# Normalising the attention output through DRAM instead of on TensorE, and a new table of places

## Chip, cores and metric

The kernel runs on one core of a Trainium2 chip. The metric is device time in microseconds (us) of one execution.

## What is computed

Six transformer layers on 4 images of 512 tokens with 256 channels and 16 heads of 16 channels, and then a mixture of 8 experts. Cut to what matters:

```python
for i in range(6):
    xn = adaln(x, cond, n1)                 # layer norm, scale and shift
    q, k, v = split(xn @ qkv_w[i].T)
    a = attn(rope(q), rope(k), v)           # softmax(q k / 4) v, head by head
    x = x + a @ so_w[i].T
    xn = adaln(x, cond, n2)                 # the same with keys and values from the context
    x = x + attn(rope(xn @ cq), rope(ctx @ ck), ctx @ cv) @ co_w[i].T
    xn = adaln(x, cond, n3)
    x = x + gelu(xn @ f1_w[i].T + f1_b[i]) @ f2_w[i].T + f2_b[i]
x = x0 + x
out = x + moe(layernorm(x))                 # top 2 of 8 experts, at most 640 rows each
```

The softmax is computed without its division: `attn` first yields, for each head, the sums of exp(score) times value and the plain sum of exp(score), and the quotient of the two is the attention output.

## The kernel before

A job is one image in one attention (self or cross): 8 jobs a layer, 48 in all. The program runs in slots; slot k works on four jobs at once. **Pass 1** of job k: 32 pairs of score products (`pass1`, L788), whose row maxima DVE takes (`maximum`, L999). **Pass 2** of job k-1: 64 shifted score products (`pass2`, L761), of which ACT takes the exponential (L837), and the value products (`pv`, L774), which gather four heads at a time in one bank (`psv`): each head has 32 rows, 16 of value sums, then one row (row 16) that is the sum of exp. ACT copies a finished group of four heads to `osum` (`copy_group`, L845). The **tail** of job k-2: quotient, output projection, addition to x. The **head** of job k+1: norm, projections to q, k, rotation, split into three bf16 parts, a trip through DRAM (`bounce`) and the loads of the stacked operands `qstack` and `kstack`.

A slot has 32 places, numbered 0 to 31, two for each of its 16 units. In a unit PE issues pass2, pass1 twice, pass2, the chunks of the even place, pass2, pv, pass2, the chunks of the odd place. A **chunk** is a piece of tail or head work that goes through one PSUM bank, `side`; there is only one such bank, so a chunk starts when the one before has been read. `SHORT_PLACES` and `LONG_PLACES` say at which place each chunk stands: `HV` value projection, `HT` transposes of the normed rows, `HQ`, `HK` projections; `T1`, `T2`, `O` the tail; in long slots (tails of cross attention, 4 slots in 8, where the feed-forward network follows) also `LT`, `F1`, `F2`. All engines run through the places in the same order, in program order on each.

The tail before: `T1`, four chunks, transposes `osum` (four 128x128 transposes each, L663); DVE takes reciprocals of the sums of exp and multiplies (L1018, L1019) into `anat`. `T2`, two chunks, transposes `anat` back (L663), ACT copies to `aT` (L890, shown in rows as `hT`, whose memory it shares). `O`, two chunks, projects (L677), DVE adds to x (L1048).

SP issues all DMAs of the layers, one after another, waiting in line for each. At the turn of a slot it waits until pass 2 of job k-1 is complete, then issues ten DMAs: the second half of the heads of `qstack` and `kstack` for the next job (`load_first(k + 1, 1)`, L515 and L517, `load_second(k + 1, 1)`, L526). They read DRAM:

```python
if j >= 2:
    sp.wait_ge(s_p2full, place.jobs(j - 2, 64) + 32 * (hf + 1))
```

`NORM_PLACES` says where DVE computes the norm: for `HT` the statistics at places 0 and 1, the Newton step at 3, the four normed tiles at 3, 3, 4, 4 (L989).

In the experts, PARTS are 16 halves of experts (384 and 256 rows). For a part, `gather_T` transposes its rows on PE, DVE copies them to `gT` (`read_T`, L1466), `hidden` multiplies by w1 (L1299), ACT applies gelu, `outputs` multiplies by w2 (L1315).

Of the kernel before, what the change touches and what calls it, by code (L numbers as in the profile page):

```python
# [29 lines left out]
P = 128  # L30
# [51 lines left out]
CHUNKS_PER_LAYER = 200  # L82
DVE_PER_LAYER = 196
# [216 lines left out]
def layers(nc, a, x, mod, ident, identb, eps, maskrow, rows, acc, s_pad):  # L300
    with ExitStack() as ctx:
# [20 lines left out]
        anat = sb("anat", [P, TT, D])  # L322
# [6 lines left out]
        nT = anat[:, :, :].rearrange("p (k a) n -> p k (a n)", k=KD)  # L329
# [6 lines left out]
        recip = sb("recip", [P, TT, H])  # L336
# [6 lines left out]

        bounce = [nc.dram_tensor(f"bounce{i}", (NPROD, D, S), BF16, kind="Internal").ap() for i in range(2)]
# [26 lines left out]

        s_full = sem("chunk_filled")
# [23 lines left out]
        def slot_chunks(k):  # L396
# [14 lines left out]
            if tail:  # L411
                put("T1", "T2", "O")
# [49 lines left out]
        def _(sp):  # L462
# [27 lines left out]

            def write_part(j, w, part):
# [97 lines left out]
        def _(pool):  # L589
# [44 lines left out]
            def slot(k, p2, p1, tail, head):  # L634
                if head:
# [15 lines left out]
        def _(pe):  # L651
# [29 lines left out]
            def side_work(k, what, c):  # L681
                if what == "T1":
                    if c == 0:
                        pe.wait_ge(s_os, place.jobs(k - 1, 4))
                    transposes(begin(k, what, c), [osum[:, g, c * P:(c + 1) * P] for g in range(4)])
                elif what == "T2":
                    if c == 0:
                        wait_read(pe, place, k, "T1", 2)
# [862 lines left out]
```

## Time and profile before

| | |
|---|---|
| time, median of 3 runs | 4453.81 us (4446.65 to 4462.31) |
| profiled execution, its own time | 4442.28 us |
| its span | 4440.6 us |
| mean granted TensorE clock | 0.962 |
| layers' slots (first pass2 to the last) | 177.8 to 4069.8 us |
| experts' loop on PE | 4246.5 to 4423 us |

The span runs from the first to the last instruction. PE is TensorE, PEld its weight loads, DVE VectorE, ACT ScalarE, POOL GpSimd, SP SyncE. A slot k begins with its first pass2 product (L761). In a row of the timeline the number in brackets is the idle time of the engine before the instruction, and what ended it. In the rows `anat` also stands for `nT`, and `hT` also for `xnat` and `aT`, which share their memory.

### The profile page before, as it was taken

How to read it: one execution, taken by the hardware profiler on the slowest of the kernel's cores; microseconds unless marked ns; L12 is line 12 of the kernel's file. 1: busy time of each engine (PE TensorE's matmuls, PEld its weight loads, DVE VectorE, ACT ScalarE, POOL GpSimd, SP SyncE). 2: the span in 40 equal slices, each digit the busy share in tenths (PEclk: the TensorE clock that was granted, in tenths of full speed). 3: DMA queues.
4: the chain of work that ended last, by engine and by line, in shares of the span. 5: the costliest groups of instructions: out<-in, count | busy, mean ns of one | idle time of the engine just before them, and what ended most of it. 6: DMA issues, size and time to landing. Idle time of an engine off the chain costs nothing. (4 is left out here: it accounts for less than half of the span.)

```text
span 4440.6 us, 68492 instructions
## 1 busy us (share of the span) xinstructions
PE 3940.5 (89%) x20630; PEld 1833.7 (41%) x20630; DVE 2907.1 (65%) x4711; ACT 2561.9 (58%) x4302; POOL 857.7 (19%) x518
## 2 busy tenths in 40 slices
PE   3699999999999999999999999999999999997467
PEld 1233344533344533345433345433345433354355
DVE  3777766677766678766678766678766677752311
ACT  1376656667666567666567665567666566654122
POOL 4312121112121112211111211111211121200133
PEclk7799999999999999999999999999999999999689
DMA  5354323244323244332244332244332344410234
GB/s 162 85 135 108 97 69 78 63 108 120 87 78 72 60 113 119 87 80 65 67 108 116 94 72 66 68 108 116 97 75 59 74 129 111 109 30 13 83 99 95
DMA packets 271578, 396.39 MB, mean 89 GB/s; under 512 B 28312, under 2 KB 218400, under 8 KB 270880
## 3 DMA queue, kind: packets, MB, share of 16 engines
q1 hardware_dynamic: 263904, 382.18, 34.1%
q0 software_dynamic: 7296, 9.51, 1.3%
q8 instruction: 196, 3.21, 0.3%
q14 instruction: 182, 1.49, 0.1%
HBM read 226.63 MB, written 170.67 MB: 89 GB/s over the span
## 5 line engine op out<-in xcount | busy, mean ns | idle before, releaser
L837 ACT ACTIVATE prob<-ps 128x512 f32<-128x512 f32 x3072 | 1768.2, 596 | 1225.2 <-PE ps L761 1207.6
L999 DVE TENSOR_REDUCE negmax<-ps 128x2 f32<-128x1024 f32 x1536 | 1836.7, 1219 | 217.6 <-PE ps L788 195.2
L761 PE MATMUL ps<-qstack,kstack 114*128 114x512 bf16 x3072 | 1162.4, 389 | 100.1 <-ACT prob L837 84.8
L774 PE MATMUL psv<-prob,v 128*32 128x512 f32 x6144 | 829.5, 612 | 0.0
L761 PEld LDWEIGHTS ps<-qstack,kstack 114*128 114x128 bf16 x3072 | 284.6, 97 | 1190.3 <-ACT prob L837 794.5
L616 POOL TENSOR_TENSOR rot<-ropep 128x512 f32<-128x512 f32 x96 | 122.5, 1276 | 2486.7 <-DVE ropep L1032 2467.7
L788 PE MATMUL ps<-kstack,qstack 49*128 49x512 bf16 x3072 | 496.8, 388 | 97.9 <-DVE negmax L999 76.8
L736 PE MATMUL side<-anat,wf 128*128 128x256 f32 x1536 | 377.1, 388 | 9.9 <-DVE hT L1037 8.9
L1037 DVE TENSOR_SCALAR hT<-side,f1b 128x256 f32<-128x256 f32 x384 | 168.2, 479 | 303.6 <-PE side L736 303.6
L747 PE MATMUL side<-wf,hT 128*128 128x256 f32 x1536 | 347.9, 379 | 2.8 <-DVE x L1044 1.6
L736 PEld LDWEIGHTS side<-anat,wf 128*128 128x128 f32 x1536 | 285.6, 192 | 65.7 <-DVE hT L1037 30.9
L747 PEld LDWEIGHTS side<-wf,hT 128*128 128x128 f32 x1536 | 291.9, 190 | 41.6 <-issue 2.4
L788 PEld LDWEIGHTS ps<-kstack,qstack 49*128 49x128 bf16 x3072 | 100.0, 94 | 457.5 <-issue 279.2
L625 POOL TENSOR_TENSOR low<-rot,parts 128x1024 bf16<-128x1024 f32 x96 | 204.7, 2132 | 379.0 <-ACT parts L876 379.0
L619 POOL TENSOR_TENSOR rot<-rot,parts 128x1024 f32<-128x1024 f32 x96 | 205.4, 2140 | 207.3 <-ACT parts L872 207.3
L1044 DVE TENSOR_TENSOR x<-x,side 128x256 f32<-128x256 f32 x96 | 40.4, 421 | 297.5 <-PE side L747 297.5
L774 PEld LDWEIGHTS psv<-prob,v 128*32 128x32 f32 x6144 | 121.6, 109 | 272.1 <-issue 245.8
L669 PE MATMUL side<-xnT,wself 128*128 128x512 f32 x384 | 195.0, 632 | 31.1 <-DVE ropep L1032 29.2
L1048 DVE TENSOR_TENSOR x<-x,side 128x512 f32<-128x512 f32 x96 | 66.0, 688 | 171.2 <-PE side L677 171.2
L663 PE MATMUL side<-ident,hT 128*128 128x128 f32 x576 | 101.3, 303 | 82.0 <-DVE hT L989 79.5
L989 DVE TENSOR_SCALAR hT<-x,mv,y 128x256 f32<-128x256 f32 x288 | 163.9, 612 | 2.6
L1031 DVE TENSOR_TENSOR ropep<-side,cos 128x512 f32<-128x512 f32 x96 | 66.4, 692 | 137.4 <-PE side L669 98.5
(158 smaller groups left out, 3722.1 us busy)
## 6 DMA issues: line engine op xcount, KB each, us to landing
bounce<-parts SPq DMA_DIRECT2D x480, 256.0 KB, 2.5
qstack<-bounce SPq DMA_DIRECT2D x384, 192.0 KB, 5.5
kstack<-bounce SPq DMA_DIRECT2D x384, 192.0 KB, 6.1
bounce<-low SPq DMA_DIRECT2D x96, 256.0 KB, 2.1
ctxT<-in_ctxT SPq DMA_DIRECT2D x24, 512.0 KB, 3.9
nw<-in_nwT SPq DMA_DIRECT2D x18, 512.0 KB, 11.3
w<-in_w SPq DMA_DIRECT2D x16, 512.0 KB, 4.8
wself<-in_wself SPq DMA_DIRECT2D x24, 256.0 KB, 4.0
```

The lines of the kernel that those rows point to most:

```text
L619: nc.gpsimd.tensor_tensor(rot[:, :, :], rot[:, :, :], parts[w][:, 0, :, :], ALU.subtract).then_inc(s_r1, 1)
L625: nc.gpsimd.tensor_tensor(low[:, :, :], rot[:, :, :], parts[w][:, 1, :, :], ALU.subtract).then_inc(s_low, 1)
L669: mm = nc.tensor.matmul(bank, w[:, k, m * P:(m + 1) * P], act_T[:, k, :], start=(k == 0), stop=(k == KD - 1))
L736: mm = nc.tensor.matmul(bank[:, i * D:(i + 1) * D], wf1[:, kk, f * P:(f + 1) * P], nT[:, kk, th * (S // 2):(th + 1) * (S // 2)], start=(kk ...
L747: mm = nc.tensor.matmul(bank[:, 0:D], hT[th][:, f, t * P:(t + 1) * P], wf2[:, f, :], start=(f == 0), stop=(f == FT - 1))
L761: nc.tensor.matmul(ps2[:, n % RING2, :], kk[0:ROWS, h, kt * P:(kt + 1) * P], q[0:ROWS, h, :], start=True, stop=True).then_inc(s_p2full, 1)
L774: mm = nc.tensor.matmul(psv[32 * i:32 * i + 32, 0, :], v[j % 2][:, kt, (HD + 1) * h:(HD + 1) * h + 32], prob[:, 4 * (u % 2) + i, :], start ...
L788: mm = nc.tensor.matmul(ps1[:, 2 * (n % 2) + e, :], qs[j % 2][rows, 8 * e + m, t * P:(t + 1) * P], ks[j % 2][rows, 8 * e + m, :], start=Tr ...
L837: nc.scalar.activation(prob[:, 4 * (u % 2) + i, :], ps2[:, n % RING2, :], ACT.Exp, scale=HD ** -0.5).then_inc(s_prob, 1)
L989: ins = nc.vector.tensor_scalar(xnat[:, t, :], x[:, TT * (j % B) + t, :], mv[:, t, 0:1], y0[:, t:t + 1], ALU.subtract, ALU.mult)
L999: nc.vector.tensor_reduce(out_at, ps1[:, 2 * (n % 2):2 * (n % 2) + 2, :], AX, ALU.max, negate=True).then_inc(s_p1free, 1)
L1037: ins = nc.vector.tensor_scalar(hT[th][:, f, :], bank[:, i * D:(i + 1) * D], f1b[:, f:f + 1], None, ALU.add)
```

## The change

The transposes T1 and T2 go. SP writes each group of `osum` to DRAM (`value_sums`), loads the sums of exp back as `den` (128x64), and the value sums as `aT`, already in the layout that the projection wants; DVE takes one reciprocal of `den` at place 4; SP writes it to DRAM (`inverse`) and loads it back 16 times repeated (`recips`, in the memory of `nT`); POOL multiplies `aT` by it in one instruction; `O` waits for that. The rest of the chunks moves to new places. In the experts the rows of a part are transposed one part earlier than before.

```diff
 SHORT_PLACES = {
-    "HV": [1, 3], "T1": [2, 4, 5, 7], "HT": [6, 8], "HQ": [9, 10], "HK": [12, 14],
-    "T2": [15, 17], "O": [19, 21],
+    "HV": [1, 3], "HT": [6, 8], "HQ": [9, 11], "HK": [13, 15], "O": [18, 20],
 }
 LONG_PLACES = {
-    "HV": [1, 3], "T1": [2, 4, 5, 7], "HT": [6, 8], "T2": [9, 10], "O": [11, 12], "HQ": [13, 14],
-    "HK": [15, 16], "LT": [17, 18], "F1": [19, 20, 21, 22, 23, 24, 25, 26], "F2": [27, 28, 30, 31],
+    "HV": [1, 3], "HT": [5, 7], "O": [8, 10], "HQ": [9, 11], "HK": [12, 13], "LT": [15, 16],
+    "F1": [17, 18, 19, 20, 21, 22, 23, 24], "F2": [26, 27, 29, 30],
 }
-SHORT_SHIFT, LONG_SHIFT = (23, 0), (29, 0)
+SHORT_SHIFT, LONG_SHIFT = (23, 0), (28, 0)
...
-    "LT": dict(stats=[12, 12, 12, 12], aggregate=13, newton=15, tiles=[15, 15, 16, 16]),
+    "LT": dict(stats=[10, 10, 10, 10], aggregate=11, newton=13, tiles=[13, 13, 14, 14]),
 }
-GUESS_PLACES = {"HT": 2, "LT": 14}
+GUESS_PLACES = {"HT": 2, "LT": 12}
+RECIP_PLACE = 4
...
-SHORT_SPLIT = (13, 15, 18, 20)
-LONG_SPLIT = (16, 18, 20, 22)
-GELU_PLACES = (23, 27)
+SHORT_SPLIT = (13, 15, 19, 21)
+LONG_SPLIT = (13, 15, 17, 19)
+GELU_PLACES = (21, 25)
...
+            def write_sums(j, g):
+                sp.wait_ge(s_os, place.jobs(j, 4) + g + 1)
+                sp.dma_start(sums[j % 2][4 * g:4 * g + 4].rearrange("h r n -> (h r) n"), osum[:, g, :]).then_inc(s_sums, 16)
+
+            def load_attention(j):
+                sp.wait_ge(s_sums, place.jobs(j + 1, 64))
+                sp.dma_start(den[:, :], sums[j % 2][:, HD].rearrange("h (c n) -> h c n", c=P // H)).then_inc(s_den, 16)
+                for k in range(KD):
+                    sp.dma_start(aT[:, k, :], sums[j % 2][8 * k:8 * k + 8, 0:HD]).then_inc(s_aload, 16)
+                sp.wait_ge(s_recip, place.jobs(j + 1, 1))
+                sp.dma_start(inverse[j % 2].rearrange("h (c n) -> (h c) n", c=P // H), recip[:, :]).then_inc(s_inv, 16)
+                sp.wait_ge(s_inv, place.jobs(j + 1, 16))
+                for k in range(KD):
+                    sp.dma_start(recips[:, k, :], inverse[j % 2][8 * k:8 * k + 8, None, :].to_broadcast([8, HD, S])).then_inc(s_aload, 16)
...
             def slot(k, p2, p1, tail, head):
                 side_done = place.at(start[k], CHUNKS_PER_LAYER)
+                if tail:
+                    sp.wait_ge(s_full, side_done)
+                    write_sums(k - 2, 3)
+                    load_attention(k - 2)
...
                 if p2:
                     shift_rows(k, k - 1, 1)
+                    write_sums(k - 1, 0)
...
                     write_and_load(k + 1)
+                if p2:
+                    write_sums(k - 1, 1)
+                    write_sums(k - 1, 2)
...
             def slot(k, p2, p1, tail, head):        # POOL
+                if tail:
+                    pool.wait_ge(s_aload, place.jobs(k - 1, 64))
+                    nc.gpsimd.tensor_tensor(aT[:, :, :], aT[:, :, :], recips[:, :, :], ALU.mult).then_inc(s_anorm, 1)
...
                 elif what == "O":
                     if c == 0:
-                        wait_read(pe, place, k, "T2", 0)
-                        wait_read(pe, place, k, "T2", 1)
+                        pe.wait_ge(s_anorm, place.jobs(k - 1, 1))
...
                     for what, c in plan[at]:
                         side_work(k, what, c)
+                    if tail and at == RECIP_PLACE:
+                        dve.wait_ge(s_den, place.jobs(k - 1, 16))
+                        nc.vector.reciprocal(recip[:, :], den[:, :]).then_inc(s_recip, 1)
...
             gather_T(0)
             hidden(0)
+            gather_T(1)
             for n in range(len(PARTS)):
                 if n + 1 < len(PARTS):
-                    gather_T(n + 1)
                     hidden(n + 1)
+                if n + 2 < len(PARTS):
+                    gather_T(n + 2)
                 outputs(n)
```

On DVE, the rows below are from place 3's Newton step to the maxima of place 5 (`negmax<-ps`) in a slot with a tail; `hT<-x,mv,y` are the normed tiles, and an `ISA` row is a wait. Before:

```order
L984 SCALAR_TENSOR_TENSOR y<-lnv,y 128x4
L956 ISA
L989 TENSOR_SCALAR hT<-x,mv,y 128x256 x2
L997 ISA
L999 TENSOR_REDUCE negmax<-ps 128x2
L436 ISA
L1018 RECIPROCAL recip<-side 128x16
L956 ISA
L1019 TENSOR_TENSOR anat<-side,recip 128x256
L989 TENSOR_SCALAR hT<-x,mv,y 128x256 x2
L997 ISA
L999 TENSOR_REDUCE negmax<-ps 128x2
```

And of the changed kernel, on the same engine at the same place:

```order
L1011 SCALAR_TENSOR_TENSOR y<-lnv,y 128x4
L983 ISA
L1016 TENSOR_SCALAR hT<-x,mv,y 128x256 x2
L1024 ISA
L1026 TENSOR_REDUCE negmax<-ps 128x2
L1100 ISA
L1101 RECIPROCAL recip<-den 128x64
L1016 TENSOR_SCALAR hT<-x,mv,y 128x256 x2
L1024 ISA
L1026 TENSOR_REDUCE negmax<-ps 128x2
```

The wait at L1100 for `den` now stands between the maxima of place 4 and the last two normed tiles, with the maxima of place 5 behind it.

On SP, the DMAs at the turn into a slot with a tail, with what each waits for; `value_sums` is the new DRAM tensor, `hT` here the `aT` in it, `nT` the `recips`. Before, from the last of the ten loads on:

```order
L526 DMA kstack<-bounce 48x2048
L436 ISA
L561 DMA ctxT<-in_ctxT 128x2x512 [waits chunk_filled]
L439 ISA
L489 DMA qstack<-mrow 2x4x512 [waits chunk_read]
L489 DMA qstack<-mrow 2x4x512
```

And of the changed kernel:

```order
L554 DMA kstack<-bounce 48x2048
L583 ISA
L504 ISA [waits chunk_filled]
L505 DMA value_sums<-osum 128x512 [waits pv_group_copied]
L509 ISA
L510 DMA den<-value_sums 128x1x64 [waits value_sums_written]
L512 DMA hT<-value_sums 128x1x512 x2
L513 ISA
L514 DMA inverse<-recip 128x64 [waits reciprocals_ready]
L515 ISA
L517 DMA nT<-inverse 128x1x512 [waits reciprocals_written]
L517 DMA nT<-inverse 128x1x512
```

The write of the last group and the chain of loads now follow directly on the ten loads, ahead of `ctxT` and `mrow`.

On PE, from the second `HT` chunk to the first `O` chunk of a long slot of the changed kernel; `hT` is `xnat` in the first and `aT` in the last row:

```order
L703 MATMUL side<-ident,hT 128x128 x4
L790 ISA
L791 MATMUL ps<-qstack,kstack 128x512
L815 ISA
L818 MATMUL ps<-kstack,qstack 128x512 x2
L815 ISA
L818 MATMUL ps<-kstack,qstack 128x512 x2
L790 ISA
L791 MATMUL ps<-qstack,kstack 128x512
L724 ISA
L698 ISA
L717 MATMUL side<-wcross,hT 128x256 x4
```

`O` (with its wait at L724) stands at place 8, where before the second `HT` chunk stood and `O` came three places later.

## Rows read from the trace of the kernel before

**Rows 1.** The page's part 1: busy us, share of the span, instructions.

```profile
PE 3940.5 (89%) x20630; PEld 1833.7 (41%) x20630; DVE 2907.1 (65%) x4711; ACT 2561.9 (58%) x4302; POOL 857.7 (19%) x518
```

**Rows 2.** Groups of instructions by line, shapes kept apart, whole run.

```profile
L663 PE MATMUL side<-ident,osum 128*128 128x128 f32 x768 | 117.0, 274 | 3.2 <-DVE anat L1019 2.4 <-ACT osum L845 0.7
...
L663 PE MATMUL side<-ident,anat 128*128 128x128 f32 x384 | 61.5, 283 | 5.8 <-ACT hT L890 2.3 <-DVE anat L1019 0.9
...
L1018 DVE RECIPROCAL recip<-side 128x16 f32<-128x16 f32 x192 | 48.2, 251 | 35.6 <-PE side L663 35.6
```

**Rows 3.** Stretches: length, busy us of each engine (count), granted clock, DMA.

```profile
1628.60:1695.00 66.40, 62.29 (x345) 22.56 (x344) 52.40 (x74) 45.94 (x82) 13.56 (x8) 1.00 0.42 104
1926.90:2023.40 96.50, 90.95 (x481) 47.11 (x480) 64.38 (x110) 57.86 (x92) 15.87 (x9) 1.00 0.27 66
2023.40:2121.40 98.00, 92.45 (x481) 47.48 (x480) 64.39 (x110) 58.08 (x92) 15.88 (x9) 0.98 0.28 66
1556.70:1628.60 71.90, 64.05 (x344) 23.05 (x345) 51.87 (x72) 45.69 (x81) 13.54 (x8) 0.98 0.47 127
```

**Rows 4.** Timeline, PE, in the short slot that begins at 1761.4.

```profile
1767.24 0.60 PE L663 MATMUL side<-ident,osum 128*128 128x128 f32 x4
1767.68 0.38 PE L761 MATMUL ps<-qstack,kstack 114*128 114x512 bf16 x1
...
1775.37 0.39 PE L788 MATMUL ps<-kstack,qstack 49*128 49x512 bf16 x2 [0.24 <-DVE negmax L999]
...
1784.89 1.98 PE L669 MATMUL side<-xnT,wcross 128*128 128x512 f32 x4 [0.40 <-DVE ropep L1032]
```

**Rows 5.** Timeline of DVE in the same slot.

```profile
1771.69 1.23 DVE L999 TENSOR_REDUCE negmax<-ps 128x2 f32<-128x1024 f32 x1 [0.56 <-PE ps L788]
...
1773.45 0.73 DVE L989 TENSOR_SCALAR hT<-x,mv,y 128x256 f32<-128x256 f32 x2
```

**Rows 6.** Timeline of SP's DMA issues in the same slot.

```profile
1761.59 0.31 SPq L515 DMA_DIRECT2D qstack<-bounce  x1
...
1766.14 0.41 SPq L526 DMA_DIRECT2D kstack<-bounce  x1
```

**Rows 7.** Line L526 in that burst: issue to landing of its four DMAs.

```profile
DMA to landing us min/median/max: 5.1/6.0/6.9
```

**Rows 8.** Line L503 in the slot before: issue to landing, 12 DMAs.

```profile
DMA to landing us min/median/max: 2.1/2.5/2.9
```

**Rows 9.** Timeline of ACT in the same slot.

```profile
1765.12 0.59 ACT L845 ACTIVATE osum<-psv 128x512 f32<-128x512 f32 x1
```

**Rows 10.** Timeline, PE, around the long slot that begins at 1926.9.

```profile
1923.40 3.62 PE L747 MATMUL side<-wf,hT 128*128 128x256 f32 x16
...
1941.57 0.66 PE L663 MATMUL side<-ident,hT 128*128 128x128 f32 x4
...
1945.12 0.60 PE L663 MATMUL side<-ident,hT 128*128 128x128 f32 x4
...
1973.91 0.65 PE L663 MATMUL side<-ident,hT 128*128 128x128 f32 x4 [2.58 <-DVE hT L989]
```

**Rows 11.** Timeline, SP, the first of the ten loads there.

```profile
1923.60 0.31 SPq L515 DMA_DIRECT2D qstack<-bounce  x1
```

**Rows 12.** Timeline of DVE and POOL in that long slot.

```profile
1968.25 2.55 DVE L989 TENSOR_SCALAR hT<-x,mv,y 128x256 f32<-128x256 f32 x2
...
1968.47 2.19 POOL L619 TENSOR_TENSOR rot<-rot,parts 128x1024 f32<-128x1024 f32 x1 [2.04 <-ACT parts L872]
```

**Rows 13.** Timeline, DVE, first slot of a layer (begins at 1556.7).

```profile
1562.93 1.23 DVE L999 TENSOR_REDUCE negmax<-ps 128x2 f32<-128x1024 f32 x1 [5.88 <-issue]
```

**Rows 14.** Timeline of PE in the last slot.

```profile
4074.98 0.66 PE L663 MATMUL side<-ident,osum 128*128 128x128 f32 x4 [0.72 <-ACT osum L845]
...
4085.07 3.75 PE L677 MATMUL side<-wcross,hT 128*128 128x256 f32 x8 [0.78 <-ACT hT L890]
```

**Rows 15.** Groups of PE's instructions by line in the experts' loop.

```profile
L1299 PE MATMUL eps<-gT,w 128*128 128x384 f32 (+1 forms) x256 | 77.1, 456 | 20.8 <-DVE gT L1466 20.8
```

More of the change, by code:

```diff
@@ L81 @@
 FT = DFF // P
-CHUNKS_PER_LAYER = 200
-DVE_PER_LAYER = 196
+CHUNKS_PER_LAYER = 152
+DVE_PER_LAYER = 164
 EXP_SET = "natural_log_exp_and_others"
@@ L327, in layers @@
         aT = hT[0][:, 0:4, :].rearrange("p (k a) n -> p k (a n)", k=KD)
-        nT = anat[:, :, :].rearrange("p (k a) n -> p k (a n)", k=KD)
+        recips = nT
         cos = sb("cos", [P, S])
@@ L335, in layers @@
         mrow = sb("mrow", [16, 2, S], BF16)
-        recip = sb("recip", [P, TT, H])
+        den = sb("den", [P, H * S // P])
+        recip = sb("recip", [P, H * S // P])
         st = sb("st", [P, TT, 6])
@@ L342, in layers @@
         fence_at = sb("fence_at", [P, 1])
+        sums = [nc.dram_tensor(f"value_sums{i}", (H, 32, S), F32, kind="Internal").ap() for i in range(2)]
+        inverse = [nc.dram_tensor(f"inverse{i}", (H, S), F32, kind="Internal").ap() for i in range(2)]
         bounce = [nc.dram_tensor(f"bounce{i}", (NPROD, D, S), BF16, kind="Internal").ap() for i in range(2)]
@@ L370, in layers @@
         s_os = sem("pv_group_copied")
+        s_sums = sem("value_sums_written")
+        s_den = sem("probability_sums_loaded")
+        s_recip = sem("reciprocals_ready")
+        s_inv = sem("reciprocals_written")
+        s_aload = sem("attention_loaded")
+        s_anorm = sem("attention_normed")
         s_full = sem("chunk_filled")
@@ L411, in slot_chunks @@
             if tail:
-                put("T1", "T2", "O")
+                put("O")
             if p1:
@@ L681, in side_work @@
             def side_work(k, what, c):
-                if what == "T1":
+                if what == "O":
                     if c == 0:
[L684 to L688, printed above, removed]
-                        wait_read(pe, place, k, "T1", 3)
-                    transposes(begin(k, what, c), [anat[:, t, c * P:(c + 1) * P] for t in range(TT)])
-                elif what == "O":
-                    if c == 0:
-                        wait_read(pe, place, k, "T2", 0)
-                        wait_read(pe, place, k, "T2", 1)
+                        pe.wait_ge(s_anorm, place.jobs(k - 1, 1))
                     w = wcross if is_cross(k - 2) else wself
@@ L840, in copy_group @@
             def copy_group(k, j, g):
-                if g == 0 and k >= 2:
-                    wait_filled(act, place, k, "T1", 3)
+                if j > 0:
+                    act.wait_ge(s_sums, place.jobs(j - 1, 64) + 16 * (g + 1))
                 act.wait_ge(s_pv, place.jobs(j, 16) + 4 * g + 4)
@@ L887, in side_work @@
                     modulate(k, what, c)
-                elif what == "T2":
-                    wait_filled(act, place, k, what, c)
-                    nc.scalar.activation(aT[:, c, :], bank, ACT.Copy).then_inc(s_read, 1)
                 elif what == "HV":
@@ L1010, in side_work @@
             def side_work(k, what, c):
-                if what not in ("T1", "HQ", "HK", "O", "F1", "F2"):
+                if what not in ("HQ", "HK", "O", "F1", "F2"):
                     return
@@ L1014, in side_work @@
                 bank = side[:, 0, :]
-                if what == "T1":
-                    heads = bank.rearrange("p (h e) -> p h e", h=H)
-                    wait_step(step(nc.vector.reciprocal(recip[:, c, :], heads[:, :, HD])))
-                    nc.vector.tensor_tensor(anat[:, c, :].rearrange("p (h d) -> p h d", h=H), heads[:, :, 0:HD],
-                                            recip[:, c, :, None].to_broadcast([P, H, HD]), ALU.mult).then_inc(s_read, 1)
-                elif what in ("HQ", "HK"):
+                if what in ("HQ", "HK"):
                     j, w = k + 1, int(what == "HK")
@@ L1477, in biased @@
                                             b2[:, e:e + 1, :].to_broadcast([P, count, D]), ALU.add).then_inc(s_yr, 1)
+            read_T(0)
+            read_T(1)
             gates(0)
-            read_T(0)
             for n in range(len(PARTS)):
-                if n + 1 < len(PARTS):
-                    if n % 2 == 1:
-                        gates((n + 1) // 2)
-                    read_T(n + 1)
+                if n + 2 < len(PARTS):
+                    read_T(n + 2)
+                    if n % 2 == 0:
+                        gates(n // 2 + 1)
                 biased(n)
```

2 lines of the change are left out of this document (1 added, 1 removed).

## Prediction

> **What bounds the kernel.** I read the busy times first: PE is busy for 89% of the span, DVE for 65%, ACT for 58% [rows 1]. An average hides stages, so next came single slots as stretches. A short slot takes 66.4 us with PE busy for 62.3, a long one 96.5 with PE busy for 91.0 [rows 3]. The layers are bound by PE almost everywhere, and what matters is PE's order: its queue is in order, so a wait of PE for one chunk or one maximum is lost time, and work taken off PE is won time unless a wait follows. Then I read the timelines of PE, DVE, ACT and SP through the first 20 us of a slot, since there the changed kernel puts a chain of transfers.
>
> **What the removed work gives.** A T1 chunk at place 2 of a short slot starts at 1767.24 and the pass2 product after it at 1767.68 [rows 4]: 0.44 us of PE. T2's products last as long (283 ns against 274 [rows 2]). Six chunks give 6 x 0.44 = 2.64 us a slot. Also the wait of 0.40 us before the second HQ chunk goes [rows 4], since HQ now stands at 9 and 11, and the 0.24 us wait for a maximum at 1775.37 is no wait when T1's work is off DVE. Where no chunk stands between two pass2 products they must wait for ACT, for which I take back 0.2 us (a choice, below the 0.44 of the chunk gone). Without any new wait a slot would gain about 3.0 us; 46 slots carry a tail beside passes 1 and 2 of other jobs, so 138 us (slots 2 to 47).
>
> **When `den` lands.** All times are from the start of a slot; the short one begins at 1761.4.
> - The ten loads of the next job's stacks are issued from +0.2 (1761.59) to +4.7 (1766.14) [rows 6]. The last lands 6.9 us after its issue [rows 7], at +11.7; in other slots this was up to half a microsecond earlier, and I take +11.5. They are bound by data: four DMAs issued in 1.4 us land with 5.1 to 6.9 us.
> - `osum`'s last group is copied at +4.3 (1765.12 plus 0.59) [rows 9], so the write of `value_sums` is issued at about +5, right behind the loads in SP's queue. Alone such a write of 256 KB takes 2.1 us [rows 8], which would be +7. Behind the loads it cannot be earlier than these; I take +12.0 (bounds +11.7, and +13, where it takes the loads' own pace).
> - `den` is issued when the write has landed. The nearest row for its 32 KB is 2.1 us for 256 KB [rows 8]. Bounds: 1.7, as it is smaller, and 2.9. I take 2.2 with the semaphore: +14.2.
>
> In today's long slots the loads are issued 3.3 us before the slot starts (1923.60 against 1926.9 [rows 11]), because the last F2 chunk of 3.6 us stands at place 31, behind the last pass2 product [rows 10]. The new table puts it at 30, ahead of that product. So this head start goes, and long slots get the same +14.2.
>
> The Trainium skill, "DMA: Bandwidth & Descriptors", Queues, rings and completion order, says that descriptors are consumed in ring order on each DMA engine, but that completion is not FIFO per issuing engine. By the first half the write lands behind the loads, by the second it could overtake some; no row here has a DMA issued during the loads' issue that lands before them.
>
> **What waits for it.** DVE ends the maxima of place 4 at +11.4 today (1771.69 plus 1.14, the step to the next instruction at 1772.83), and 0.4 earlier without T1 at place 2: +11.0 [rows 5]. There it now waits for `den`, 3.2 us. Queued behind that wait are the last two normed tiles and the maxima of place 5. The reciprocal of 64 elements: 16 take 251 ns [rows 2]; at some 0.16 fixed and 5.5 ns each I get 0.5 (bounds 0.25 and 1.0). Two tiles 0.65 (1773.45 to the next at 1774.09), a maximum 1.13.
> - **Short slot.** The second pass1 product of unit 3 needs the maxima of place 5: 14.2 + 0.5 + 0.65 + 1.13 + 0.1 = +16.6. Today it starts at 1775.37, +14.0 [rows 4]. So PE is 2.6 us later there than today. After it come the savings not yet used: three of the six chunks (1.3) and the 0.4, less 0.2: 1.5. Net +1.1 us a slot.
> - **Long slot.** The first HT chunk, now at place 5, needs the normed tiles: 14.2 + 0.5 + 0.65 + 0.1 = +15.45. From there to place 8 are three places: two places with two small chunks take 3.55 us (1941.57 to 1945.12 [rows 10]), bare 2.65, so three bare ones 4.0, and with 0.9 for both HT chunks O is reached at +20.35. But O waits for POOL's product: the reciprocal is there at +14.7; `inverse` lands 2.2 later, +16.9; the two `recips` loads are issued 0.4 apart and land after 2.5 (median of 256 KB [rows 8]), +19.9; POOL's product of 128x1024 float32 takes 2.19 as today's L619 [rows 12]: +22.1, with semaphores +22.3. Today the second HT chunk is at this place, at +18.2 (1945.12 [rows 10]). PE is 4.1 later; one HT and two T2 chunks and 0.2 of a wait are still to be saved, 1.6. Net +2.5.
>
> The bounds together (den 1.0 earlier or 1.8 later, the transfers of `inverse` and `recips` each 0.4 less or 1 more) move a slot by about -1 to +2 us.
>
> **Other parts.** The LT wait of 2.6 us [rows 10] comes from DVE's normed tiles, which took 2.55 instead of 0.73 us while POOL ran its 2.19 us instruction [rows 12, 5]. The same instructions stay neighbours (LT 5 places behind the second O as before): nothing. The new POOL product runs when no normed tiles are due: nothing; if tiles met it, up to 1.8 a slot. The Trainium skill, "SBUF — State Buffer", section on its two separate sides, calls the pair shared by VectorE and GpSimd an exclusive lock held for the whole instruction; the row agrees, and by it POOL's product is free only between DVE's norm stages. `mrow` and `ctxT`, now issued behind the chain at about +17 instead of +10, are needed from the HK chunks on, behind HQ's second, which today starts at +23.5 (1784.89 [rows 4]): hidden. The first slot of a layer (four times; 71.9 us [rows 3]) has DVE 5.9 us late anyway [rows 13], which hides the wait: there -2.6.
>
> Last two slots: without pass 1 nothing else covers the chain. In the last one the sums are copied at 4074.98 and O starts at 4085.07 [rows 14], 10.1 later; new 2.1 + 2.2 + 0.5 + 2.2 + 2.9 + 2.3 = 12.2, so +2; the slot before reaches O with the chain still running, +4 (bounds 1 and 7).
>
> Clock: two long slots differ by 98.0 and 96.5 us, with PE's mean granted clock 0.98 and 1.00 and the waits alike [rows 3]: a spell at 1.2 GHz costs 1.4. In the first slot of a layer, after 5 us of idle, the clock is 0.98 too. PE idles 3 to 4 us at once in each new slot. I take a spell in 6 of 10 short slots and one more in half the long ones: 12 x 1.4 + 11 x 1.4 = 32 (bounds 0 and 90).
>
> Experts: PE waits 20.8 us for `gT` [rows 15]. With the rows transposed and copied one part ahead, these waits are covered by 3 to 5 us of `outputs`: -20.
>
> **Sum.** 20 short slots x 1.1 = +22; 4 first slots x -2.6 = -10; 22 long x 2.5 = +55; ends +6; clock +32; experts -20: +85. Against the profiled execution's 4442.3 us this is 4527. The median of the runs shown is 11.5 higher, so the forecast is **4539 us**.
>
> **Rivals.**
> - *Forecast: DVE waits for `den` in nearly every slot, and O in the long ones* (0.62). 4450 to 4620.
> - *`den` is in time, on the faster side* (0.16). It must land by +11, which asks that the write overtakes the loads. Then short slots win 3.0, and long ones still wait for O: 11 + 0.5 + 2.2 + 3.0 + 2.3 = +19.1, reached at 16.7, so 0.5 won. 20 x -3 - 10 - 22 x 0.5 + 6 - 20 = -95: 4359. It decides the sign as soon as `den` lands before about +12.4.
> - *The waits cost what is won* (0.12). `den` at +13: the short slots -0.1, the long ones +1.3, no clock spells: -20 - 10 + 29 + 4 - 2 = about 0: 4440 to 4467.
> - *The chain costs more* (0.10): the loads through DRAM at 5 to 7 us as the stacks' loads [rows 7], the half clock in every slot: +160 to +200, 4630.
>
> Against the first speaks nothing but the queue's order not being proven for this write; against the last, that `value_sums` and `recips` have large rows like the 2.1 to 2.9 us transfers.
>
> **Numbers.** A range of 4430 to 4610 leaves out most of the fast rival and the last: 2 in 10. What a measurement can tell from no change is 0.3%, 13 us. Slower: the forecast's 0.62, the last rival's 0.10, a third of the 0.12: 0.76. Same 0.06, faster 0.18.
>
> **What the changed profile would show.** DVE's RECIPROCAL at place 4 with 3 us of idle before it, ended by the DMA of `den`; pass1 waiting 2 to 4 us for maxima in short slots, HT for normed tiles in long ones; O's first chunk waiting about 2 us for POOL in long slots; no wait for `gT`. Short slots of 67 to 69 us, long ones of 98 to 101. The prediction is wrong if the write of `value_sums` lands before the ten loads, or if DVE reaches the reciprocal later than +14.

## The result, and the profile after

The changed kernel takes 4701.9 us (median of 4, 4696.17 to 4707.3) against 4454.35 for the kernel before in the same session (4446.65 to 4462.31): ratio 1.0555, interval 1.0531 to 1.058. The forecast was 4539 us with a range of 4430 to 4610. The sign came as forecast, and the loss is about three times as large. The profiled execution's span is 4705.6 us, so 265 us more than the 4440.6 before.

The page's part 1 of the changed kernel, busy us and share of the span:

```profile
PE 3948.3 (84%) x19478; PEld 1741.9 (37%) x19478; DVE 2832.6 (60%) x4375; ACT 2512.0 (53%) x4206; POOL 970.1 (21%) x566
```

PE has 1152 instructions fewer than in [rows 1], and is busy 7.8 us longer. The chunks that went were worth 0.44 us each in place [rows 4], 6 x 48 x 0.44 = 127 us, so the work that stayed became about 135 us slower. And PE's idle time went from 4440.6 - 3940.5 = 500 us to 4705.6 - 3948.3 = 757. These two are the loss: idle +257, slower work +135, removed work -127.

What the idle time is shows in the waits of PE (us in all, times, longest):

```profile
PE ps L791 <- ACT prob L867: 151.6, 238, 2.3
PE side L717 <- POOL hT L674: 117.1, 24, 17.6
PE side L703 <- DVE hT L1016: 111.3, 40, 19.3
PE ps L791 <- DMA qstack<-mrow: 80.3, 22, 8.0
PE ps L818 <- DVE negmax L1026: 69.6, 72, 7.8
```

The same view of the kernel before has 84.8 us for `prob`, 79.5 for the normed tiles, 76.8 for the maxima, 4.0 for `mrow` (once) and nothing for POOL. So: POOL's product +117, `mrow` +76, `prob` +67, normed tiles +32, maxima -7. With -19 of waits for `ropep` and -20 of waits for `gT` that is +246 of the 257.

Stretches of the changed kernel, in the columns of [rows 3]: a short slot, the first of a layer, and two long slots.

```profile
1796.50:1865.20 68.70, 61.68 (x321) 20.41 (x321) 49.73 (x66) 44.97 (x80) 15.88 (x9) 0.98 0.51 133
1656.70:1727.50 70.80, 61.58 (x321) 20.96 (x321) 50.03 (x68) 45.12 (x81) 15.89 (x9) 0.97 0.62 174
2039.80:2145.90 106.10, 92.96 (x458) 45.19 (x456) 64.31 (x104) 56.80 (x90) 18.21 (x10) 0.95 0.32 81
2145.90:2253.20 107.30, 93.03 (x458) 45.43 (x456) 64.26 (x104) 56.80 (x90) 18.22 (x10) 0.95 0.31 80
```

The short slot is 2.3 us longer than the 66.4 of [rows 3], the two long ones are 9 to 10 longer. The long ones also have the lower clock, 0.95 against 0.98 to 1.00, and PE busy for 93.0 us where 458 instructions should take less than the 481 before (91 to 92.5).

**The chain in a long slot.** The slot that begins at 2039.8 on SP, from the last of the ten loads on:

```profile
2044.62 0.42 SPq L554 DMA_DIRECT2D kstack<-bounce  x1
2045.25 0.34 SPq L505 DMA_DIRECT2D value_sums<-osum  x1
2052.32 0.61 SPq L510 DMA_DIRECT2D den<-value_sums  x1
2052.97 1.25 SPq L512 DMA_DIRECT2D hT<-value_sums  x2
2055.12 0.34 SPq L514 DMA_DIRECT2D inverse<-recip  x1
2058.66 1.21 SPq L517 DMA_DIRECT2D nT<-inverse  x2
```

On DVE there, the reciprocal at place 4 (the last two normed tiles follow at 2055.01, for 0.64 us):

```profile
2054.54 0.55 DVE L1101 RECIPROCAL recip<-den 128x64 f32<-128x64 f32 x1 [3.28 <-DMA den<-value_sums]
```

On PE, the last product before the first wait, the first `HT` chunk, and the first `O` chunk:

```profile
2052.03 0.39 PE L791 MATMUL ps<-qstack,kstack 114*128 114x512 bf16 x1
2055.78 1.11 PE L703 MATMUL side<-ident,hT 128*128 128x128 f32 x4 [3.36 <-DVE hT L1016]
...
2066.25 1.99 PE L717 MATMUL side<-wcross,hT 128*128 128x256 f32 x8 [3.35 <-POOL hT L674]
```

And POOL's product between them:

```profile
2063.78 2.34 POOL L674 TENSOR_TENSOR hT<-hT,nT 128x1024 f32<-128x1024 f32 x1 [61.62 <-DMA nT<-inverse]
```

Read as distances from the slot's start: the write of `value_sums` has landed at +12.5 (forecast +12.0), `den` lands at +14.7 (+14.2), DVE had idled 3.28 us (3.2), `HT` starts at +15.96 (+15.45). Up to there the forecast holds within half a microsecond in this slot. Then it fails: `inverse` is under way for 3.54 us (forecast 2.2), from the issue of `recips` to POOL's start are 5.12 us (2.9), and `O` starts at +26.4 (+22.3).

This is the picture of the 15 long slots that follow a long one, where DVE waits 3.1 us for `den` in the mean. Over the whole run it waits for `den` in 26 slots of 48, 80.5 us in all; in the 18 short ones the mean is 0.4 us, since `den` lands there at about +12.1 of the slot, 2.1 us sooner than forecast.

**The slot's start.** The turn into the slot before that one, on SP; `mrow` holds the rows of maxima that the shifted products need:

```profile
1925.70 0.82 SPq L505 DMA_DIRECT2D value_sums<-osum  x2
1926.65 1.36 SPq L500 DMA_DIRECT2D qstack<-mrow  x2
```

and PE at the same turn:

```profile
1929.71 0.39 PE L791 MATMUL ps<-qstack,kstack 114*128 114x512 bf16 x1
1934.04 0.39 PE L791 MATMUL ps<-qstack,kstack 114*128 114x512 bf16 x1 [3.94 <-DMA qstack<-mrow]
```

`value_sums` is written here twice (groups 1 and 2, 256 KB each) right ahead of `mrow`. The slot starts 3.9 us late, before any of the chain that the prediction worked out. In the kernel before, the same turn on SP was

```profile
1821.97 1.36 SPq L489 DMA_DIRECT2D qstack<-mrow  x2
```

for a slot that starts at 1827.8: `mrow` was issued 5.8 us ahead of the product that needs it, and here 3.45 us (1926.65 against 1934.04 - 3.94).

### The profile page after: what moved, and what is told of

It reads as the page before. It is cut to its first block and busy times, and to the rows that moved or that the text cites. A ratio compares the mean times of both kernels' runs of the same rounds, so it can differ in the third digit from the quotient of the medians.

```text
span 4705.6 us, 66013 instructions
## 1 busy us (share of the span) xinstructions
PE 3948.3 (84%) x19478; PEld 1741.9 (37%) x19478; DVE 2832.6 (60%) x4375; ACT 2512.0 (53%) x4206; POOL 970.1 (21%) x566
## 5 line engine op out<-in xcount | busy, mean ns | idle before, releaser
L804 PE MATMUL psv<-prob,v 128*32 128x512 f32 x6144 | 863.2, 635 | 0.7 <-ACT prob L867 0.7
L674 POOL TENSOR_TENSOR hT<-hT,nT 128x1024 f32<-128x1024 f32 x48 | 112.6, 2346 | 2400.8 <-DMA nT<-inverse 2400.8
L766 PE MATMUL side<-nT,wf 128*128 128x256 f32 x1536 | 381.2, 392 | 9.9 <-DVE hT L1058 8.9
L766 PEld LDWEIGHTS side<-nT,wf 128*128 128x128 f32 x1536 | 290.6, 194 | 66.5 <-DVE hT L1058 30.6
L717 PE MATMUL side<-wcross,hT 128*128 128x256 f32 x384 | 130.3, 498 | 126.2 <-POOL hT L674 117.1
L1069 DVE TENSOR_TENSOR x<-x,side 128x512 f32<-128x512 f32 x96 | 65.8, 685 | 238.9 <-PE side L717 238.9
```

What stands on the lines that cost most here:

```text
L717: mm = nc.tensor.matmul(bank[:, i * D:(i + 1) * D], act_T[:, k, t * P:(t + 1) * P], w[:, k, :], start=(k == 0), stop=(k == nk - 1))
L766: mm = nc.tensor.matmul(bank[:, i * D:(i + 1) * D], wf1[:, kk, f * P:(f + 1) * P], nT[:, kk, th * (S // 2):(th + 1) * (S // 2)], start=(kk ...
L804: mm = nc.tensor.matmul(psv[32 * i:32 * i + 32, 0, :], v[j % 2][:, kt, (HD + 1) * h:(HD + 1) * h + 32], prob[:, 4 * (u % 2) + i, :], start ...
```

## Experiments

Each was timed beside the kernel before on the same chip. That kernel's median was 4449.66 us for the first four experiments and 4451.49 for the others, 3 to 5 us below the 4454.35 beside which the changed kernel was timed; so a difference against the changed kernel is good to about 5 us. In the later kernels the same line has a number one or two higher. Mean us by kind of slot, slots 2 to 42; a long slot with a short one before it stands apart, since it starts with the `mrow` wait:

| slots | before | after | sixteen | ten loads behind | long late | all together |
|---|---|---|---|---|---|---|
| short (16) | 66.4 | 69.1 | 68.8 | 68.2 | 68.9 | 66.8 |
| first of a layer (5) | 70.4 | 71.4 | 70.5 | 67.9 | 70.5 | 65.8 |
| long behind a short one (5) | 98.1 | 105.2 | 103.0 | 105.2 | 98.5 | 97.3 |
| other long (15) | 97.6 | 108.3 | 104.7 | 103.4 | 98.1 | 96.5 |

### The experts' part alone

```diff
+            gather_T(1)
             for n in range(len(PARTS)):
                 if n + 1 < len(PARTS):
-                    gather_T(n + 1)
                     hidden(n + 1)
+                if n + 2 < len(PARTS):
+                    gather_T(n + 2)
```

(with the same shift in DVE's `read_T`), in the kernel before.

> The kernel before with the experts' part of the change alone (rows transposed and copied one part earlier). Theory: PE's 20.8 us of waits for gT in the experts' loop go nearly whole, as in the trace after (1.3 left), so 19 us less than before, ratio 0.996. Rival: the loop is bound by POOL's adds or by the loads of rows, and less than 10 us come out.

4431.55 us, ratio 0.9957 (0.9941 to 0.9974): -18 us, as expected. In the changed kernel the group of [rows 15] reads

```profile
L1323 PE MATMUL eps<-gT,w 128*128 128x384 f32 (+1 forms) x256 | 73.4, 441 | 1.3 <-DVE gT L1493 1.3
```

1.3 us of waits for 20.8. The term of -20 holds, and the attention part alone is then worth some +265.

### `mrow` ahead of the two writes

```diff
-                if p2:
-                    write_sums(k - 1, 1)
-                    write_sums(k - 1, 2)
                 if p1:
                     shift_rows(k, k, 0)
+                if p2:
+                    write_sums(k - 1, 1)
+                    write_sums(k - 1, 2)
```

> The changed kernel with SP's issue of mrow (first half) ahead of the two writes of value_sums that stand before it. Theory: in the 19 short and first long slots of a layer PE's 3 to 4 us wait for mrow at the slot's start is due to those 512 KB; without them it falls to under 1.5 us, but the slot then starts earlier against its ten loads, and part of the gain comes back as DVE's wait for den: 20 to 45 us less than the changed kernel in all. Rival A: mrow waits for the ten loads themselves, which the table moved later, and the order of the writes changes under 10 us. Rival B: nothing comes back, 60 us or more.

4681.5 us, ratio 1.0516 (1.0497 to 1.0535): 20 us less than the changed kernel, at the lower edge of what was expected. PE's waits in this run:

```profile
PE ps L818 <- DVE negmax L1026: 84.2, 69, 6.6
PE ps L791 <- DMA qstack<-mrow: 48.0, 22, 8.4
```

and the same turn of the slot, SP and then PE:

```profile
1917.09 1.36 SPq L500 DMA_DIRECT2D qstack<-mrow  x2
```

```profile
1923.88 0.39 PE L791 MATMUL ps<-qstack,kstack 114*128 114x512 bf16 x1 [2.53 <-DMA qstack<-mrow]
```

The wait for `mrow` falls from 80 to 48 us, some 2.2 us each and not under 1.5, and the waits for maxima rise from 70 to 84: a slot that starts earlier meets the wait for `den` instead (DVE's mean wait for it in short slots rises from 0.4 to 1.35 us). So about 40% of the `mrow` time is due to the two writes' place, and some of what is won there goes to the next wait.

The first rival of the expectation accounts for the rest. In short slots `mrow` is issued 6.9 us ahead of its use in the kernel before, 3.6 in the changed kernel and 4.6 here (means of 18). The writes' place is 1.0 of the 3.3 us lost. The other 2.3 come with the ten loads ahead of `mrow` (the first half of the heads for the next job): the last of them is issued 7.4 us ahead of the slot's start before, and 5.1 in both others. In the short slots' table `HK` stands at 13 and 15 where it stood at 12 and 14, and what is written to DRAM for these loads comes later with it. No run put the short slots' table back, so this is read from the issue times and was not tried.

### The reciprocal at place 7

```diff
-RECIP_PLACE = 4
+RECIP_PLACE = 7
```

> The changed kernel with DVE's reciprocal (and its wait for den) at place 7 instead of 4. Theory: in long slots the chain of transfers to O ends when it ends; the 3.4 us that PE waits for the normed tiles go, and the wait for O's first chunk grows from 3.4 to 6 or 7 us, so the time stays within 30 us of the changed kernel. Rival (the step of my prediction that DVE's wait is a loss of its own): 50 us or more come out.

4711.93 us, ratio 1.0589 (1.057 to 1.0608): 10 us more. The first `O` chunk of the same slot as above:

```profile
2084.06 3.78 PE L717 MATMUL side<-wcross,hT 128*128 128x256 f32 x8 [8.50 <-POOL hT L674]
```

The first `HT` chunk no longer waits there (of 5.1 us of waits for normed tiles in this slot the 1.8 before `LT` are left), and the wait for POOL grew from 3.4 to 8.5, where 6 or 7 were expected. The slot starts at 2057.7, so `O` starts at +26.4, exactly as in the changed kernel. Two waits in a row on one chain are one loss: DVE's wait at place 4 cost little of its own in long slots, because `O` would have waited for it anyway.

### Sixteen rows outermost in the four loads

```diff
-sp.dma_start(aT[:, k, :], sums[j % 2][8 * k:8 * k + 8, 0:HD])
+sp.dma_start(aT[:, k, :], sums[j % 2][8 * k:8 * k + 8, 0:HD].rearrange("h r n -> r h n"))
-sp.dma_start(recips[:, k, :], inverse[j % 2][8 * k:8 * k + 8, None, :].to_broadcast([8, HD, S]))
+sp.dma_start(recips[:, k, :], inverse[j % 2][None, 8 * k:8 * k + 8, :].to_broadcast([HD, 8, S]))
```

The bytes are the same; the source is walked with the 16 channels of a head outermost instead of the 8 heads. The rows of the output projection's weights are permuted to match.

> The changed kernel with the loads of aT and recips written with the 16 rows of a head as the outermost dimension, not the 8 heads (the rows of the output weights are permuted to match, outside the kernel's timed part). In the trace after these loads move at half the packet rate of the write of value_sums (48 packets of 2 KB in half a microsecond against 85), as if on 8 of 16 DMA engines. Theory: with 16 as outermost dimension they take half the time; inverse lands in 2.5 instead of 3.5 us, recips 1.5 us sooner, and O's wait in long slots falls from 3.4 to under 1 us, 50 to 90 us less in all. Rival: DRAM reads of repeated rows or the fixed time of a transfer set it, and less than 15 us come out.

4628.02 us, ratio 1.0405 (1.0388 to 1.0423): 74 us less than the changed kernel, within what was expected. First the changed kernel while the two loads of `aT` run (two stretches of one microsecond), and while the ten loads and `value_sums` run (the last row); the last three columns are the granted clock, the share of the 16 DMA engines that is busy, and GB/s:

```profile
2055.50:2056.50 1.00, 0.72 (x4) 0.73 (x5) 1.00 (x2) 0.00 (x0) 0.00 (x0) 0.50 0.60 217
2056.50:2057.50 1.00, 1.00 (x5) 0.26 (x5) 0.28 (x1) 0.32 (x1) 0.00 (x0) 0.50 0.52 197
...
2046.00:2049.00 3.00, 2.99 (x17) 1.75 (x18) 2.82 (x7) 1.94 (x5) 0.00 (x0) 1.00 0.99 167
```

and with 16 rows outermost, at the same point of the slot:

```profile
2024.50:2025.50 1.00, 0.79 (x5) 0.60 (x5) 1.00 (x2) 0.00 (x0) 0.00 (x0) 0.76 0.99 263
```

With 8 outermost the loads keep little more than half of the engines busy, with 16 all of them. The last slot has no ten loads in it and so shows the chain nearly bare; in both kernels a write of 650 KB for the experts is issued right behind the `recips`. SP in the changed kernel there:

```profile
4365.10 0.32 SPq L514 DMA_DIRECT2D inverse<-recip  x1
4368.41 1.21 SPq L517 DMA_DIRECT2D nT<-inverse  x2
```

and the start of `O` behind it:

```profile
4377.05 3.78 PE L717 MATMUL side<-wcross,hT 128*128 128x256 f32 x8 [17.60 <-POOL hT L674]
```

The same two places in this experiment, SP and then PE:

```profile
4285.07 0.33 SPq L514 DMA_DIRECT2D inverse<-recip  x1
4287.48 1.16 SPq L517 DMA_DIRECT2D nT<-inverse  x2
```

```profile
4294.52 3.78 PE L717 MATMUL side<-wcross,hT 128*128 128x256 f32 x8 [15.07 <-POOL hT L674]
```

From the issue of `inverse` to `O` are 11.95 us with 8 rows and 9.45 with 16. `inverse` itself, the same 32 KB in both, takes 3.31 and 2.41 us: it stands behind the loads of `aT`, so their pace is its pace too. By the forecast's terms (2.2 + 2.9 + 2.3) it should have been 7.4. Even with all engines 2 us are missing, and the 650 KB write is not what makes them: from the issue of `recips` to POOL's start are 4.65 us in this slot, and 4.5 in the mean of the 15 long slots, where only the small `mrow` loads follow. That two loads of 256 KB run side by side fits the rows and was not tried by itself. `O`'s wait in long slots did not fall under 1 us as expected, but from 4.1 to 2.4 in the mean.

The Trainium skill, "DMA: Bandwidth & Descriptors", states the rule under Why a DMA increments its semaphore by 16 and not by 1, and again in its Rules for kernel authors: the number of engines follows from the slowest dimension of the two patterns that isn't 1, and an outermost size below 16 confines the transfer to at most that many. The trace agrees, with 0.52 to 0.60 of the engines against 0.99. The prediction drew on another section of that page, and its terms lacked this one.

### The long slots' table of before

```diff
 LONG_PLACES = {
-    "HV": [1, 3], "HT": [5, 7], "O": [8, 10], "HQ": [9, 11], "HK": [12, 13], "LT": [15, 16],
-    "F1": [17, 18, 19, 20, 21, 22, 23, 24], "F2": [26, 27, 29, 30],
+    "HV": [1, 3], "HT": [6, 8], "O": [11, 12], "HQ": [13, 14], "HK": [15, 16], "LT": [17, 18],
+    "F1": [19, 20, 21, 22, 23, 24, 25, 26], "F2": [27, 28, 30, 31],
 }
-SHORT_SHIFT, LONG_SHIFT = (23, 0), (28, 0)
+SHORT_SHIFT, LONG_SHIFT = (23, 0), (29, 0)
```

`LT`'s norm, the splits and the gelus go back with it to their places before, and SP waits for group 0's write before it issues those of groups 1 and 2. T1 and T2 stay away, and the chain through DRAM stays.

> The changed kernel with the long slots' places of before (O at 11 and 12 and not 8 and 10, the last F2 chunk at 31 and not 30), the rest of the change kept. Theory: the ten loads of the next slot start 3.3 us sooner again, so den lands by +12 in the slots that follow a long one, DVE's wait there falls from 3.3 to under 1 us, and O, reached some 5 us later, waits under 1 us where it waited 3.4; with fewer spells at the low clock long slots fall from 108 to 96 to 99 us, 180 to 240 us less in all, which is near the time of the kernel before. Rival: ACT's waits and the low clock have another cause, and under 120 us come out.

4487.53 us, ratio 1.008 (1.0063 to 1.0097): 214 us less than the changed kernel, by a table of places alone. PE's waits:

```profile
PE ps L792 <- ACT prob L868: 98.8, 201, 1.1
PE ps L819 <- DVE negmax L1027: 81.8, 99, 7.8
PE side L704 <- DVE hT L1017: 80.8, 24, 19.3
PE ps L792 <- DMA qstack<-mrow: 79.1, 22, 8.0
...
PE side L718 <- POOL hT L675: 23.8, 9, 16.6
```

POOL from 117 to 24 us (16.6 of them in the last slot), normed tiles back to 81, `prob` from 152 to 99. That is -177 of waits, less what the maxima (+12) and `ropep` (+11) take back, and PE's busy time falls from 3948.3 to 3884.0 with the same 19478 instructions: -64. A whole long slot then is

```profile
2058.00:2154.80 96.80, 89.21 (x458) 44.47 (x456) 62.44 (x103) 56.87 (x90) 18.25 (x10) 1.00 0.36 89
```

So the early place of `O`, which asks for the chain's result before it can be there, together with the places that went with it, was most of the loss. The run doesn't part the three things that come back with this table: `O` stands behind the chain; the last `F2` chunk at place 31 gives the ten loads their head start again, so that DVE reaches the reciprocal at +11.7 and waits 0.2 us for `den` where it was +14.5 and 3.1 (means of 15 slots); and the gelus are back at places with chunks. The short slots, which this edit doesn't touch, stay at 68.9.

### Both: late long slots and sixteen rows

The two edits above together (with the wait for group 0's write).

> The one before together with the sixteen-engine loads of aT and recips. Theory: once O stands late enough the chain is hidden, so the faster loads bring only what is left in the last two slots and in the first long slot of a layer: 5 to 20 us less than with the late places alone. Rival: the loads hinder others (bounce, stacks) by their engines' share, and 40 us or more come out.

4463.74 us (median of 10), ratio 1.0024 (1.0014 to 1.0033): 24 less than with the late table alone, a little more than the 5 to 20 expected; with the early table the same loads were worth 74. Once `O` stands behind the chain, its length counts a third as much. This version is 0.24% slower than the kernel before, and the experts' part gives it 18 us, so the attention part alone still costs about 30.

### The ten loads behind the chain

```diff
                 if p2:
                     shift_rows(k, k - 1, 1)
+                if p1 and k > 0:
+                    load_first(k, 1)
+                    load_second(k, 1)
+                if p2:
                     write_sums(k - 1, 0)
...
-                if head:
-                    load_first(k + 1, 1)
-                    load_second(k + 1, 1)
```

in the changed kernel with its own table (and the wait for group 0's write): the last group of `value_sums` no longer has the ten loads ahead of it.

> The changed kernel, its places kept, with the ten loads of the stacks' second half issued behind the chain for the attention output (in the next slot, behind mrow) and not ahead of it. Theory: they are why den is late; now den lands by +9.5 of a slot, DVE waits for it nowhere, the 3.4 us of PE before the first HT chunk in long slots go, O waits for POOL about 5 us since it is reached sooner, and PE's wait for mrow at the start of short slots stays at 2 to 4 us: 40 to 100 us less than the changed kernel. Rival: den is late by its own transfers, and its landing moves by under 1 us.

4593.22 us, ratio 1.0319 (1.0302 to 1.0337): 109 us less than the changed kernel, somewhat more than expected. SP in the same long slot, which begins at 2004.4 here:

```profile
2008.71 0.33 SPq L505 DMA_DIRECT2D value_sums<-osum  x1
2010.77 0.59 SPq L510 DMA_DIRECT2D den<-value_sums  x1
...
2016.28 0.32 SPq L514 DMA_DIRECT2D inverse<-recip  x1
2017.72 1.21 SPq L517 DMA_DIRECT2D nT<-inverse  x2
```

and POOL:

```profile
2024.08 2.34 POOL L676 TENSOR_TENSOR hT<-hT,nT 128x1024 f32<-128x1024 f32 x1 [57.38 <-DMA nT<-inverse]
```

The same write takes 2.06 us instead of 7.07, and `inverse`, with nothing ahead of it, 1.44 instead of 3.54. `den` is there 6 us earlier, the waits for normed tiles go back to 63.6 us in the run, and those for maxima to 47.3. But DVE comes to place 4 only at +11.5, so `inverse` is issued at +11.9 (+15.3 in the changed kernel), and the `recips` take 6.36 us from issue to POOL, with `mrow` and the ten loads issued right behind them. `O` starts at +22.1 for +26.4, and still waits 4.1 us, since PE reaches it earlier too. So the burst of loads is what made `den` late, and moving it away leaves `O`'s early place as it was.

### All together

The late table, sixteen rows, the ten loads behind the chain and `mrow` ahead of the writes (and the wait for group 0's write).

> The changed kernel with all four: late places in long slots, sixteen-engine loads, mrow ahead of the writes, ten loads behind the chain. Theory: no wait for den, POOL or mrow is left, the 2.6 us of T1 and T2 a slot come out of PE's time: short slots 64 us, long ones 93 to 95 us, in all 4300 to 4350, faster than both kernels. Rival: the waits move to the stacks' loads (the second half would be late for pass 1 in the middle of the slot), and it stays above 4400.

4379.4 us, ratio 0.9839 (0.9821 to 0.9857): faster than both kernels: 72 us (1.6%) less than the kernel before, of which the experts' part is 18. It missed what was expected by 30 to 80 us. PE on the page, and then its waits:

```profile
PE 3834.3 (88%) x19478; PEld 1711.4 (39%) x19478; DVE 2796.1 (64%) x4375; ACT 2511.8 (57%) x4206; POOL 970.7 (22%) x566
```

```profile
PE ps L793 <- ACT prob L869: 98.8, 201, 1.1
PE side L705 <- DVE hT L1018: 80.8, 24, 19.3
PE ps L820 <- DVE negmax L1028: 64.2, 92, 6.6
...
PE ps L793 <- DMA qstack<-mrow: 49.9, 22, 6.9
```

Of the waits for POOL 15.4 us are left, nearly all in the last slot. A long slot:

```profile
2005.50:2100.90 95.40, 88.87 (x457) 44.48 (x456) 62.39 (x103) 56.87 (x90) 18.24 (x10) 1.00 0.37 90
```

The long slots won 1.1 of the 2.64 us that T1 and T2 took out, the short ones nothing (66.8 against 66.4). What keeps them from winning all of it is, against the kernel before, 46 us more of waits for `mrow`, 14 more for `prob` and 21 of slower work. The `LT` wait of 2.6 us [rows 10] is in every long slot of both kernels, and could be won besides. The first slots of a layer won 4.6.

## Why the prediction was right in direction and wrong in size

In the order of its steps:

- **When `den` lands: right for 15 long slots, not for short ones.** In a long slot behind a long one +14.7 for +14.2. The write behind the loads took 7.07 us and landed at +12.5. The loads behind the chain show the cause: the same write takes 2.06 us when they are not ahead of it. The rival in which the write overtakes the loads is out. In short slots `den` landed at +12.1, because these slots themselves start some 3 us late (below) while SP's queue runs on.
- **DVE's wait: right in size where it occurs, absent in short slots.** 3.28 us for 3.2 in the long slot, and `HT` at +15.96 for +15.45; in long slots the prediction let `O`'s wait cover it, and the reciprocal at place 7 confirms that: the wait vanished, `O` started at the same +26.4, and the time did not fall. But "DVE waits for `den` in nearly every slot" holds in 26 of 48, and the short slots' +1.1 rested on it. Their +2.7 has another cause.
- **The step that failed first: `inverse` lands in 2.2 us and `recips` in 2.5 to 2.9.** They took 3.54 and 5.12 in the slot above. The sum has no term for the two `aT` loads (512 KB), which are issued ahead of `inverse`, and it took the duration of the `recips`, which are loads, from writes to DRAM [rows 8]. Three things are in it, of which the runs show two: the four loads used half of the DMA engines (-2.5 us for the chain in the last slot when they use all, 74 us in all); `inverse` stood behind the loads of `aT` (1.44 us with nothing ahead of it); and the third, argued only, is that two loads of 256 KB run side by side (4.5 us on all engines for the 2.9 forecast). The rival "the chain costs more", given 0.10, named this. `O` was 8.2 us later and not 4.1, which by the prediction's own terms makes +6.6 of its +2.5. Measured were +10.7 in fifteen long slots and +7.1 in five; the rest is the waits for `prob` (+2.4 to +2.9 a long slot) and the clock, both below.
- **"`mrow` ... hidden": wrong.** The prediction looked at the `mrow` loads of the slot's middle and left out those at its end, and with them the writes of groups 1 and 2, which it never priced. Before, PE waited for `mrow` once, 4.0 us; now 22 waits take 80 us, mostly 3 to 4 each. Short slots lose 2.7 us a slot, not 1.1, and most of it here. With `mrow` ahead of the writes 32 us of this go and DVE's wait for `den` comes back in short slots. Most of the 48 us left go with the ten loads ahead of `mrow`, which the short slots' table issues 2.3 us nearer to the slot's start. This is read from the issue times.
- **"Where no chunk stands ... 0.2 us": about right in short slots, too small in long ones.** `prob` waits rose by 67 us, and 53 of them went with the long table of before. In the 18 short slots they rose from 45.0 to 46.9 us in all. In the long slot above two of 1.13 and 1.57 us end at +74 and +88, each behind a gelu on ACT. The first is there before too (1.13); the second is new, with no chunk beside this gelu, where an `F2` chunk of 3.6 us stood before. That the gelu's place causes it was read from the rows and not tried by itself.
- **The clock: right in kind, a quarter of the size.** 32 us were taken, bounds 0 and 90. PE's busy time for the same 19478 instructions is 3948.3 us in the changed kernel, 3884.0 with late long slots and 3834.3 with all together. Against 3813 (before, less 127) the changed kernel's is +135. The prediction counted 23 spells more at 1.4 us each. The trace's clock record has, between the first and the last pass2 product, 16 spells at 0.50 (1.2 GHz) before, 75 us in all, and 79 after, 380 us: 63 more, at 2.1 us each. Of the 79, 21 begin within a wait for `mrow` or 1.5 us behind it, 21 so at a wait for POOL and 18 at one for normed tiles. In the slot above the four `HT` transposes take 1.11 us behind the wait of 3.36, and 0.60 in the next chunk. Not every such wait brings one: behind the wait of 3.35 for POOL in the same slot `O` starts at the full clock:

```profile
2066.00:2067.00 1.00, 0.75 (x4) 0.68 (x4) 0.00 (x0) 0.00 (x0) 0.12 (x1) 1.00 0.00 0
```

| against the kernel before, us | idle | at 0.50 | slower work |
|---|---|---|---|
| changed kernel | +257 | +305 | +135 |
| `mrow` ahead | +246 | +271 | +124 |
| reciprocal at 7 | +292 | +344 | +109 |
| sixteen | +201 | +234 | +111 |
| ten loads behind | +189 | +159 | +84 |
| long late | +102 | +165 | +70 |
| late and sixteen | +87 | +152 | +62 |
| all together | +40 | +38 | +21 |

The slower work is 0.3 to 0.6 of the time at the low clock, and 0.4 to 0.7 of the idle time. It doesn't follow the idle time alone: with the reciprocal at place 7 one long wait stands for two short ones, PE idles 35 us more than in the changed kernel and its work is 26 us less slow. No run changed the clock alone, so that the waits bring the spells stays an inference from where the spells begin and from this table.
- **The ends: +6, measured +16.** From the start of slot 48 to the last `O` are 92.3 us before and 108.5 after: slot 48 went from 77.0 to 89.2 us, and the last chain, from the copied sums (4359.57 + 0.60) to `O`, took 16.9 us for the 12.2 forecast. Slot 47, which the prediction counted among its 22 long ones, went from 85.8 to 98.8.
- **Experts: right.** -20, measured -18 alone.
- **The first slots of a layer: -2.6 forecast, +1.0 measured.** DVE's own late start hid most of the wait, as said (waits for maxima fell from 3.7 to 2.9 us a slot); but ACT's waits rose from 2.5 to 4.3, and there are 8 spells at 0.50 in the six of them for 3.

So the sum had the experts right, and DVE's wait in the long slots, and three terms too small: the transfers from `inverse` to `recips` and with them `O`'s wait in long slots (2 us a slot forecast, 4.1 measured, 117 us of POOL waits in all), the slot's end (0 forecast, 76), and the clock (32 forecast, 135). A fourth, the waits for `prob` in long slots, was put at 0.2 and came to over 2. In the short slots the sign was luck: the term rested on the wait for `den`, and `mrow` made the loss.

## What to carry to other kernels

Price a chain through DRAM transfer by transfer, in the order of its queue: what is issued ahead of each one, how many engines its outermost dimension allows, and how many of its kind run at once. Here durations read from transfers of the same size with another shape and direction came out too short. When work moves into a queue, list all its DMAs at the turn of the slot, the ones of the other jobs too, since a small load behind large loads and writes can start the slot late. And first move the consumer behind the chain, then shorten the chain: the long slots' table (with all that it moved) was worth 214 us, the faster loads 74 before it and 24 after.

## What was not expected of the hardware

- Loads whose outermost dimension is 8 keep 0.52 to 0.60 of the DMA engines busy at some 200 GB/s; the same bytes with 16 outermost 0.99 at 263 GB/s.
- A write of 32 KB takes 1.44 us with nothing ahead of it, 2.41 behind two loads on all engines and 3.31 to 3.54 behind two on half of them: most of the smaller transfer's duration is what stands ahead of it.
- Idle time of PE that came mostly in waits of 3 to 4 us, spread over the slots (+257 us), went with 63 more spells at a granted clock of 0.50 and +135 us of slower matmuls, about half its length again; fewer and longer waits (+292 us) went with +109.
